# Masked graph attention on one core: five row buffers, constants on a second queue, eight adjacency chunks, a column-tiled first layer

## What is computed

```python
h = relu(layernorm(x))
neib_att = tanh(neigh @ Wn1 + bn1) @ Wn2 + bn2        # 256 -> 32 -> 32
value    = neigh @ Wv + bv                            # 256 -> 128
x_att    = tanh(h @ Wx1 + bx1) @ Wx2 + bx2            # 256 -> 32 -> 32
ws = leaky_relu(x_att @ neib_att.T, 0.01)             # 4096 x 4096
ws = softmax(where(adj > 0, ws, -9e15), axis=1)
out = x + concat([h @ Wfx + bfx, ws @ value], axis=1)
```

## Time and profile before

| | us |
|---|---|
| median of 3 runs | 514.41 (512.79 to 516.66) |
| the profiled execution | 515.66 |
| its span, first to last instruction | 513.9 |

### The profile page before, as it was taken

The page is one execution under the profiler, slowest core; times in us unless marked ns, Lnnn a source line. Parts: engine busy times, 40 slices in busy tenths (PEclk is TensorE's granted clock), DMA queues, the critical chain, the costliest instruction groups (busy, mean ns, idle before and its releaser), DMA issues.

```text
span 513.9 us, 8883 instructions
## 1 busy us (share of the span) xinstructions
PE 479.7 (93%) x2813; PEld 368.3 (72%) x2855; DVE 432.8 (84%) x843; ACT 436.2 (85%) x625; POOL 214.0 (42%) x340
## 2 busy tenths in 40 slices
PE   5797889799999999999999999999999999998996
PEld 4354667577878777877787778777777787766884
DVE  1559979789989998999998999899998989984654
ACT  2645699999989998999999989998999989996552
POOL 1602113235654456455654564456444544440100
PEclk8879999999999999999999999999999999999999
DMA  6854885565545844575566636655575456500100
GB/s 179 197 159 115 147 156 89 115 116 93 83 81 102 168 75 73 121 164 83 83 119 133 106 61 122 139 104 84 103 144 84 79 81 138 90 5 0 42 1 22
DMA packets 38530, 52.07 MB, mean 101 GB/s; under 512 B 4436, under 2 KB 30292, under 8 KB 38484
## 3 DMA queue, kind: packets, MB, share of 16 engines
q0 software_dynamic: 9216, 33.56, 40.3%
q1 hardware_dynamic: 29268, 17.95, 11.8%
HBM read 80.86 MB, written 4.19 MB: 166 GB/s over the span
## 4 chain that ended last, share of the span: by engine, by line
PE 68%; issue 6%; ACT 4%; DVE 2%; POOL 1%; DVEq 0%; ACTq 0%; POOLq 0%
PE ps_turned L916 20%; PE ps_scores L893 10%; PE ps_product L935 10%; PE ps_product L937 10%; PE ps_product L936 10%; PE ps_scores L892 3%; ACT pt_hi L504 2%; PE ps_product L861 2%; DVE pt_lo L674 1%; ACT scores L528 1%; PE ps_product L839 1%; PE ps_product L853 1%; POOL scores L416 1%; PE ps_product L846 1%; PE ps_product L946 1%
## 5 line engine op out<-in xcount | busy, mean ns | idle before, releaser
L674 DVE TENSOR_TENSOR pt_lo<-ps_turned,pt_hi 128x512 fp32r<-128x512 f32 x256 | 172.3, 685 | 36.7 <-ACT pt_hi L504 20.8
L416 POOL TENSOR_TENSOR scores<-scores,mask 128x512 f32<-128x512 f32 x109 | 127.8, 1173 | 170.6 <-ACT scores L528 170.4
L504 ACT ACTIVATE pt_hi<-ps_turned 128x512 fp32r<-128x512 f32 x256 | 157.1, 615 | 33.7 <-PE ps_turned L916 32.6
L916 PE MATMUL ps_turned<-ident,scores 128*128 128x128 f32 x1024 | 156.3, 275 | 2.9 <-DVE pt_lo L674 2.5
L916 PEld LDWEIGHTS ps_turned<-ident,scores 128*128 128x128 f32 x1024 | 121.7, 140 | 48.4 <-DVE pt_lo L674 25.7
L528 ACT ACTIVATE scores<-ps_scores 128x1024 f32<-128x1024 f32 x128 | 133.2, 1040 | 8.9 <-PE ps_scores L893 8.7
L893 PE MATMUL ps_scores<-neib,xs 128*128 128x512 f32 x256 | 135.5, 538 | 2.7 <-DVE mask L661 2.3
L540 ACT ACTIVATE scores<-scores,neg_top 128x2048 f32<-128x2048 f32 x64 | 129.4, 2022 | 0.0
L692 DVE CUSTOM_DVE_ANT_0 scores<-ps_scores,scores,top 128x1024 f32<-128x1024 f32 x96 | 122.6, 1277 | 3.1 <-issue 1.4
L935 PE MATMUL ps_product<-pt_hi,v_hi 128*128 128x512 f32 x256 | 113.2, 442 | 0.2 <-DVE pt_lo L674 0.2
L937 PE MATMUL ps_product<-pt_lo,v_hi 128*128 128x512 f32 x256 | 101.2, 396 | 0.0
(11 more groups left out here) (77 smaller groups left out, 380.6 us busy)
## 6 DMA issues: line engine op xcount, KB each, us to landing
adj_in<-in_adj POOLq DMA_DIRECT2D x64, 512.0 KB, 5.5
scores<-in_L_gnn_neigh SPq DMA_DIRECT2D x8, 512.0 KB, 5.5
x_rows<-in_x SPq DMA_DIRECT2D x8, 512.0 KB, 5.5
x_left<-in_x SPq DMA_DIRECT2D x8, 256.0 KB, 2.9
x_right<-in_x SPq DMA_DIRECT2D x8, 256.0 KB, 4.4
out_h<-x_left SPq DMA_DIRECT2D x8, 256.0 KB, 2.7
out_h<-x_right SPq DMA_DIRECT2D x8, 256.0 KB, 4.5
scores<-in_x SPq DMA_DIRECT2D x1, 512.0 KB, 3.9
```

The lines of the kernel that those rows point to most:

```text
L416: pool.tensor_tensor(half, half, mask[:, s % MASK_RING, BANK:CHUNK], ALU.add).then_inc(masked, 1)
L504: act.activation(pt_hi[:, (2 * b + u) % HI_RING], pt[:, u], ACT.Copy).then_inc(hi_done, 1)
L674: dve.tensor_tensor(pt_lo[:, u], pt[:, u], pt_hi[:, (2 * b + u) % HI_RING].bitcast(FP32), ALU.subtract).then_inc(lo_done, 1)
L916: last = pe.transpose(pt[:, u, i * P:(i + 1) * P], scores[:, parity * TILES + i, n * P:(n + 1) * P], ident[:, :])
```

## The change

- **Rows.** `rows` becomes a ring of five buffers; group e waits only for the turn of group e-5. SP's first DMAs are rows 0, rows 1, the first x rows, rows 2, then four DMAs of `w2_n`, rows 3 and 4, four of `w2_x`, `x_ahead`, rows 5 to 7.
- **Constants.** `w1_n` (now 32 columns wide, not repeated), `w1_x`, both `b1` and both `b2` are loaded by six DMAs that ScalarE issues ahead of its first copy. The waits are split: `w1_in`, `b1_in`, `b2_in`, `w2_in`.
- **Layers.** The first layer is 8 matmuls of 32x128 in four column tiles (`first_layer`): 128 rows of the group per tile, one tile per 32 partitions. `hidden` is 128x128; the rounded copy, the remainder and `w2_stack` are gone. The second layer is 4 float32 matmuls of 128x128 with a block-wise `w2_n`. `att_high` moves from VectorE to ScalarE.
- **Adjacency.** Chunks 4 to 7 get a place of their own (`adj_front`, in the scores of tile 3), and GpSimd issues the four first loads as rows 4, 5, 6 and 7 land (`PACE`). Chunks 8 to 11 are loaded at steps 0 and 2; from step 8 on the loads go out as before.
- **x.** The turn of the first x group moves from e = 1 to e = 5. The step numbers of the x work change.
- **Order in a step.** TensorE: both scores come first and side goes ahead of product(-1). ScalarE: hi(0) ahead of aggregate, side ahead of power. VectorE: x work, negate, close and the value's low part between lo(0) and lo(1).

```diff
-X_LOAD = -10
-X_STATS = (-6, -6, -5, -4)
+X_LOAD = -8
+X_STATS = (-6, -6, -6, -4)
 X_AGGR = -4
-X_RSTD = (-2, -2, -1, -1)
-X_NORM = (0, 2, 4, 4)
-X_TURN = (6, 7)
-X_FIRST, X_TANH = 9, 11
-X_SECOND = (13, 13)
+X_RSTD = (-3, -2, -1, -1)
+X_NORM = (0, 1, 2, 4)
+X_TURN = (6, 8)
+X_FIRST, X_TANH = 9, 10
+X_SECOND = (11, 13)
 X_STACK = (13, 14)
-X_WIDE, X_LEFT = (15, 16, 18, 19), 19
-X_LEFT_LOAD, X_SUM = 4, (8, 18)
-X_RIGHT = 8
+X_WIDE, X_LEFT = (15, 17, 19, 19), 19
+X_LEFT_LOAD, X_SUM = 11, (10, 13)
+X_RIGHT = 7
...
-            for e in range(2, NEIGH_GROUPS):
-                sp.wait_ge(turned, KT * (e - 1))
+            for e in range(ROWS_RING, NEIGH_GROUPS):
+                sp.wait_ge(turned, KT * (e - ROWS_RING + 1))
                 load_neigh(e)
...
-            for n in range(0, ADJ_RING, LOAD):
-                load_adj(n, 0)
+            for n, e in zip(range(0, ADJ_RING + FRONT, LOAD), PACE):
+                pool.wait_ge(rows_in[e % ROWS_RING], 16 * (e // ROWS_RING + 1))
+                load_adj(n)
...
-                n = s - LOAD + 2 + ADJ_RING
-                if n % LOAD == 0 and ADJ_RING <= n < STEPS:
-                    pool.wait_ge(mask_done, n - ADJ_RING + LOAD)
-                    load_adj(n, n // CHUNKS)
+                n = s + ADJ_RING + (FRONT if s < FRONT else 0)
+                if s % LOAD == 0 and n < STEPS and not FRONT <= s < ADJ_RING + FRONT:
+                    pool.wait_ge(mask_done, s + LOAD)
+                    load_adj(n)
...
+            for side, w, b, c, w_in, b_in, c_in in ((0, w1_n, b1, b2, wn1, bn1, bn2), (1, w1_x, b1, b2, wx1, bx1, bx2)):
+                act.dma_start(w[:, :, :], w_in.rearrange("(k p) h -> p k h", p=P)).then_inc(w1_in[side], 16)
...
             def step(s):
+                hi(s, 0)
                 aggregate(s)
-                hi(s, 0)
                 rise(s)
                 hi(s, 1)
+                side(s)
                 power(s)
-                side(s)
...
                 lo(s, 0)
+                x_work(s)
+                negate(s)
                 close(s)
-                negate(s)
-                x_work(s)
+                neigh_rest(s)
                 lo(s, 1)
                 if POOL_MASKS <= s < STEPS - 2:
                     mask_of(s + 2)
-                neigh_rest(s)
...
+            def first_layer(q):
+                pe.wait_ge(turned_out, KT * (q + 1))
+                if q == 0:
+                    pe.wait_ge(w1_in[0], 16)
+                wait(pe, hidden_done, q)
+                for k in range(KT):
+                    for i in range(TILES):
+                        last = pe.matmul(ps_hidden[i * D_HID:(i + 1) * D_HID, :], w1_n[:, k, :],
+                                         rows_t[:, q, k * GROUP + i * P:k * GROUP + (i + 1) * P],
+                                         start=k == 0, stop=k == KT - 1)
+                last.then_inc(first_done, 1)
...
                 wait(pe, att_out, q - 1)
-                pe.matmul(ps_att[par], w2_stack, hidden_stack[:, par], start=True, stop=True).then_inc(second_done, 1)
+                for i in range(TILES):
+                    last = pe.matmul(ps_att[par][:, i * P:(i + 1) * P], w2_n[:, i, :], hidden[:, par],
+                                     start=True, stop=True)
+                last.then_inc(second_done, 1)
...
             def step(s):
                 score(s, 0)
+                score(s, 1)
                 turn(s, 0)
-                score(s, 1)
                 product(s, -2)
                 turn(s, 1)
+                side(s)
                 product(s, -1)
                 agg_turn(s)
-                side(s)
```

More of the change, by code:

```diff
@@ L56 @@
 DMA_RING = 512
-CONSTS_IN = 16 * 4, 16 * 6
+ROWS_RING = 5
+FRONT = 2 * LOAD
+TURN_X = 5
+PACE = (4, 5, 6, 7)
+B1_IN = 16 * 2
+W2_IN = 16 * TILES
 B2_IN = 16 * 2
@@ L191, in build @@
         adj_ready = [sem(f"adj_ready{i}") for i in range(ADJ_RING // LOAD)]
+        front_ready = [sem(f"front_ready{i}") for i in range(FRONT // LOAD)]
         mask_done = sem("mask_done")
@@ L249, in load_neigh, with load_w2 @@
             def load_neigh(e):
-                par = e % 2
-                sp.dma_start(rows[:, par], neigh_tiles[:, bass.ds(e * TILES, TILES), :]).then_inc(rows_in[par], 16)
+                slot = e % ROWS_RING
+                sp.dma_start(rows[slot], neigh_tiles[:, e * TILES:(e + 1) * TILES, :]).then_inc(rows_in[slot], 16)
+            def load_w2(side, w, w_in):
+                for j in range(TILES):
+                    sp.dma_start(w[j * D_HID:(j + 1) * D_HID, j, :].rearrange("p (r h) -> p r h", h=D_HID),
+                                 w_in.rearrange("p (a h) -> p a h", a=1).to_broadcast(
+                                     [D_HID, P // D_HID, D_HID])).then_inc(w2_in[side], 16)
             def load_x_rows(e):
@@ L520, in rise @@
                 act.wait_ge(scored, s + 1)
+                if s == (TILES - 1) * CHUNKS:
+                    act.wait_ge(mask_done, ADJ_RING + FRONT)
                 if s == GSTEPS:
+                    act.wait_ge(turned, KT * NEIGH_GROUPS)
                     act.wait_ge(second_done, NEIGH_GROUPS)
```

155 lines of the change are left out of this document (65 added, 90 removed).

## The result

The changed kernel takes 505.6 us (median of 4 runs, 505.19 to 506.33) where the kernel before, on the same chip, takes 515.5 (4 runs, 512.79 to 517.51). The ratio is 0.9837, with a 95% interval of 0.9808 to 0.9867, so some 8 us gained (9.9 between the medians, 10.3 between the profiled executions, 515.66 and 505.33). The forecast was 495, with 486 to 507 as its range: the direction and the range held, and under half of the forecast gain of 20 came.

A forecast was written before the change was run, and what follows sets the result against it. The prediction took the prologue as bound by what SP issues and when, the long stage by TensorE. Gains of 13.3 + 2.2 + 4.7 = 20.2 from 515.66 gave 495.5, stated as 495 us, range 486 to 507.

The forecast's parts named there:

- Term 1: Prologue: first score starts at 34 instead of 47.28, gaining 13.3 us; bounds 30.6 and 40.7 for its start.
- 3.4 us of waits left: Prologue: allowance for rows 1 and 2, `x_ahead` statistics and four normalisations, added to 30.6 for a first score at 34.
- Term 2: First main-loop steps: two biases and a remainder leave VectorE around step 0, gaining 2.2 us; bounds 0 and 2.2.
- Eight chunks: 0 to 1: First stage: eight adjacency chunks loaded ahead gain 0 to 1 us, as no long wait was found there.
- Term 3: Long stage: GpSimd's Newton part 0 a step earlier gains 0.79 in each of six groups, 4.7 us; bounds 0 and 6.
- Term 4: Long stage: everything else, reordered steps with the same instructions and 0.49 us of slack, costed at 0; bounds -6 and +10.
- C: Rival, long stage: x rows land late and VectorE stands still, 2 us in six groups, 507 us; chance 0.10.
- A: Rival, prologue: it starves again, first score at 40.7, 501.5 us; chance 0.19 together with E.
- B: Rival: first score at 31 and x's split second layer spares half a microsecond in six groups, 488 to 489; chance 0.17.
- D: Rival, main loop: turn(0) behind the second score delays the leak, about 0.3 us per step, 527 us; chance 0.07.
- E: Rival, prologue: moving constants does nothing since rows land late, not SP's issue; near 501; chance 0.19 together with A.
- no or one stretch of clock 0.50: Prologue: sign that the forecast is right, TensorE's granted clock falling to half at most once.

The follow-up runs named there:

- p_ahead_late: old_steps_rstd with x constants issued after ScalarE's first two copies, `b1` waited by side, `x_ahead` and `w2_x` loaded behind all rows, `x_ahead` statistics later: 496.52 us.
- old_steps: Changed kernel's prologue, constants and adjacency, with the step orders and `X_` numbers of the kernel before: 505.14 us, ratio 0.9846.
- p_one_ring: p_ahead_late with four adjacency chunks in one ring, as in the kernel before, in place of eight in two: 502.33 us, ratio 0.9771.
- old_steps_rstd: old_steps with one number changed, `X_RSTD` (-3, -2, -1, -1), so Newton part 0 comes one step earlier: 499.07 us, ratio 0.9745.
- p_x_rows_late: p_ahead_late with the first two masks a prologue step earlier and the first x rows loaded behind the fourth group's rows: 498.54 us, ratio 0.9668.
- p_consts_sync: p_ahead_late with the first two masks a prologue step earlier and the six constants issued by SyncE again: 508.39 us (three runs), ratio 0.9814.

## Why the prediction was right in direction and twice too large

Its sum was 13.3 + 2.2 + 4.7 + 0 = 20.2 us. Between the two profiles it came out as 9.0 + 1.6 and some 6 gained and some 6 lost in the long stage, 10.4.

**Term 1, the first score: 13.3 forecast, 9.0 measured** (47.28 to 38.30). What binds was read rightly: going back to two buffers costs 6.6 us, and from 18 us on TensorE runs near the forecast distance. The step that was mis-sized is "3.4 us of waits left": against the 30.6 without any wait, 38.30 leaves 7.7. It left out six DMA issues and a table load ahead of ScalarE's first copy, costed "at nothing" because ScalarE is busy 9.9 of 14.4 us; that cover lies behind 32.8 us, while the issues stand at 0.7 to 6.5. The fast rate of landing that it took, 1.35 us per load, didn't come either: the third group's load, the fourth issued, goes out at 2.31 and the group is turned only at 11.7 even with the way free. The statistics of `x_ahead` ahead of VectorE's first attention half were named within the 3.4, without a price of their own. And the central value had no half speed in it, while TensorE's instructions up to 18 us are of that length: the turns at 4.83, 8.50 and 13.86 take 0.9 us more each than the later ones. The signs agree: the second group's turn, due by 10 us, starts at 8.50, the third's only at 13.86. Taking the delays away step by step brought the first score to 37.73, 36.04 and 35.52; of these only the step to 36.04 (p_ahead_late) is larger than the scatter of 1.3. The starting point was bad as well: one of the two stretches at half clock in the earlier trace rows was not there in another execution of the same prologue.

**Term 2, first steps: 2.2 forecast, 1.6 measured** between the first and the seventeenth relu; with the old orders and numbers (old_steps) it is 2.3, so the term was right and the new steps take 0.6 of it. "Eight chunks: 0 to 1" was the error beside it. In the kernel before, with its first relu at 48.36, adjacency seemed hidden; p_one_ring prices the second ring at 5.8 us once the prologue is short. A cover was costed in the old schedule although the change itself takes it away.

**Term 3, Newton part 0: 4.7 forecast.** Right, and low: 1.13 to 1.17 us per group, some 6 us, alone on either kernel. The row of 0.79 was one group; the whole wait of ScalarE, 6.7 in 6, was the better measure.

**Term 4, orders and numbers: 0 forecast, about 6 lost** (505.6 against 499.07 us in old_steps_rstd). This is the step that failed. "The same instructions" and 0.49 us of slack per step say nothing about the step in which VectorE takes three statistics or ScalarE waits for TensorE's x work. In the profile of after, VectorE takes the statistics in step 10 of a group, and a low part and a mask follow ahead of the leak, which comes at 221.22. The last line is GpSimd's, its sum for x of the same step:

```profile
218.50 1.07 DVE L595 BATCH_NORM_STATS2 stats<-x_rows 128x6 f32<-128x256 f32 x3
219.48 0.68 DVE L674 TENSOR_TENSOR pt_lo<-ps_turned,pt_hi 128x512 fp32r<-128x512 f32 x1
220.07 1.22 DVE L663 TENSOR_SCALAR mask<-adj_in 128x1024 bf16<-128x1024 bf16 x1
221.22 1.27 DVE L692 CUSTOM_DVE_ANT_0 scores<-ps_scores,scores,top 128x1024 f32<-128x1024 f32 x1
...
220.26 0.74 POOL L345 TENSOR_TENSOR x_left<-x_left,b_fx 128x256 f32<-128x256 f32 x1
```

The mask of the same step in p_ahead_late, where this sum stands elsewhere:

```profile
215.25 0.42 DVE L668 TENSOR_SCALAR mask<-adj_in 128x1024 bf16<-128x1024 bf16 x1
```

TensorE's score behind the leak at 221.22 waits 0.62 us. The third statistic is 0.33 of the delay (1.07 against 0.74 us for two), the stretched mask 0.80. It recurs: from 94 to 400 us TensorE waits nine times for the leak by more than 0.3 us, five times by 0.59 to 0.62 behind a mask of 1.20 to 1.22 in step 10, and four times by 0.36 to 0.39 behind one of 1.01 to 1.03 in step 12, always beside a sum of GpSimd. `X_SUM` and `X_RIGHT` put the sums there. So much of the loss probably is these two, which the prediction didn't look at and no run changes alone; what is shown is that orders and numbers together cost it. The bound of +10 that stood beside the 0 held it; the value taken didn't.

**The rivals.** C is nearest by time (507 us), and that is luck: in after the x rows land 3.7 us after their issue (median) and VectorE doesn't wait for them in the long stage. The cause of A, a prologue that starves, is part of the truth, and the measured time lies between the two. B's split second layer is in a set of numbers that together cost 0.6 us per group instead of sparing 0.5; alone it wasn't run. D's mechanism exists, at about an eighth of its deciding price. E is partly true: the third group does land late though it is issued early. But TensorE's wait of 4.52 us for constants is gone; part of it came back as ScalarE's wait of 4.28 for a bias, as its queue was the wrong place for all six.

## What to carry to other kernels

Cost a DMA issue where it stands, on the engine and in the microseconds in which it stands, and ask of each semaphore that counts several transfers which of them its waiter needs; a 512-byte bias held this prologue in three kernels. When a change shortens one stage, work out again what was hidden behind it. Moving one part of a chain a step earlier was worth 6 us beside the 9 of a new prologue, but each other number of such a table has to be tried alone, since "same work, other order" cost between 0.3 and 1.7 us per group here. And look at what runs beside an instruction on the other engines, not only at what stands ahead of it.

## What the hardware did that was not expected

- A mask of VectorE (128x1024, bf16) takes 0.41 to 0.48 us with nothing of GpSimd beside it, 53 times in the profile of after from 94 to 450 us. All 18 that take 0.70 or more there, up to 1.22, have an instruction of GpSimd beside them. Most masks beside a mask addition still take 0.42, so overlap alone doesn't decide it, and what does stays open.
- Small transfers beside large ones land late. The x side's `b2` (128 pieces of 4 bytes) landed about 9 us after its issue had ended in p_x_rows_late, and 12 in p_consts_sync, with DMA shares of 1.05 and 1.11 in between. It went through ScalarE's queue in the one and SyncE's in the other, and was late in both. The Trainium skill says (DMA: Bandwidth & Descriptors, Rules for kernel authors) that spreading DMAs over issuing engines only saves issue time. These two runs don't contradict it, but neither moves the same transfer alone.
- In after an issue takes ScalarE 0.5 to 1.6 us: the six on ScalarE took 5.7, with the three longest of them broadcast biases.
- In the profile of after the granted clock stands at 1.00 from the start, while eight transposes take 1.94 to 1.97 us until 17 us, the length that goes with 0.50 in the earlier trace rows. Where the column and the length of the same instructions differ, I read the length. The prediction's sign of "no or one stretch of clock 0.50" thus can't be read from the column here.
- The old prologue, profiled twice, differed by 3.0 us, nearly all of it where TensorE's clock had fallen behind a wait in one (3.23 us) and not in the other (2.37). The changed one, profiled eight times, differed by 1.3. A single profile of such a stage is one draw.
